# A graph layer's row gathers with an explicit index bound that skips, in place of the default check that reports

## Chip, cores and metric

One core of a Trainium2 chip runs the whole kernel. The time is device microseconds from the first to the last instruction of that core; lower is better. A core has five engines that run their own instruction queues: PE (TensorE), DVE (VectorE), ACT (ScalarE), POOL (GpSimd) and SP (SyncE), and 16 DMA engines that move the data. A DMA is issued from the queue of SP, ACT or POOL. A gather with indices (DMA_INDIRECT) is issued on POOL, which works on it while it is prepared; the data then move on the DMA engines.

## What is computed

A graph has N = 12,500 nodes with 128 features and E = 400,000 edges, sorted by their destination. Every edge has a source, a destination and 32 features.

```
h = relu(layernorm(x))                          # 12500 x 128
e = concat(h[src], h[dst], edge_attr)           # 400000 x 288
m = relu(e @ w1 + b1) @ w2 + b2                 # message of each edge
agg = segment_sum(m, dst)                       # 12500 x 128
out = x + GRU(agg, h)                           # three gates, h is the state
```

The product with the part of w1 that belongs to the source doesn't depend on the edge, so the kernel computes p = h @ w1_src once for each node and gathers rows of p. w2 is applied after the sum.

## The kernel before

**First stage.** x is read in 14 batches of 7 tiles of 128 nodes, normalised by DVE, POOL and ACT, transposed by PE, and multiplied with the source part of w1. The rows of p go to the DRAM tensor `p_rows`, which has NPAD = 12,544 rows of 128 floats (512 bytes each).

**Edge stage.** The edges are worked on in 625 groups of 640 edges; 5 groups make a chunk, and there are 125 chunks. The counter `s` (0 to 4) is the group's place in the chunk and names its buffers: `idx[:, s]`, `rows[:, s]`, `lhs[:, s]`, `onehot[:, s]`. For each group:

- SP loads 5 columns of 128 source indices into `idx` (line 310), after the gathers that used the buffer before have landed, and the edge features into `lhs` (line 333).
- POOL issues 5 gathers, one for each tile of 128 edges (`t` = 0 to 4, line 421): partition k of `rows[:, s, t]` gets the row of `p_rows` that `idx[k, s, t]` names. Ahead of the five it waits for the stored `p_rows`, for the indices (`idx_in`) and for the last reader of the buffer (`seg_ready`). POOL does nothing else in this stage. The loop over the chunks turns on POOL's own queue with register arithmetic and a branch; chunks 0 to 3 are written out ahead of it.
- DVE compares destinations with a row of numbers and so builds a one-hot matrix of the window of 95 nodes that the group's destinations lie in (`onehot`, line 788). PE transposes it (line 1001), multiplies the window's rows of h with the destination part of w1 (line 1004), and adds up destination part, edge features and bias in one product for each tile (line 1015).
- DVE adds that to the gathered rows (line 796), which is the step that waits for the gathers. ACT applies the relu (line 578), PE sums by destination with the one-hot matrix (line 1028), and DVE adds the sums to `acc` and `low` (lines 805, 806).
- The gates of 100 nodes at a time are computed between the groups, two chunks behind.

The order on each engine is written out by hand in a function `chunk` for each; the semaphores `rows_in[s]`, `pre_ready[s]`, `seg_ready[s]` and their kind hold them together.

**The other branch.** If some group's destinations don't fit the window, all engines take the branch `general()` instead, which is not executed with these inputs. Its scatter already carries `bounds_check=NPAD - 1, oob_is_err=False`, because it writes duplicates to an index beyond the tensor on purpose.

Of the kernel before, what the change touches and what calls it, by code (L numbers as in the profile page):

```python
# [17 lines left out]
NPAD = NT * P  # L18
# [39 lines left out]
def gnn_kernel(nc, x, src_cols, dst_cols, dst_rows, src_tiles, dst_tiles, ea_t, w1, b1, w2, b2, w_ih, b_ih, w_hh, b_hh, out):  # L58
# [7 lines left out]
    with ExitStack() as ctx:  # L66
        def sb(name, shape, dt=F32):
            return ctx.enter_context(nc.sbuf_tensor(name, shape, dt))
# [4 lines left out]
        def sems(name, n):  # L73
            return [sem(f"{name}{i}") for i in range(n)]
# [39 lines left out]
        idx = sb("idx", [P, G, T], I32)  # L114
# [88 lines left out]
        idx_in, ea_in, rows_in, h_win_ready = (sems(n, G) for n in ("idx_in", "ea_in", "rows_in", "h_win_ready"))  # L203
# [19 lines left out]
        def wait(eng, s, value):  # L223
            if not (isinstance(value, int) and value <= 0):
                eng.wait_ge(s, value)  # L225
# [146 lines left out]
        def _(pool):  # L372
# [35 lines left out]
            def chunk(c):  # L408
                arrived = c * 16 + 16
                if not isinstance(c, int):  # L410

                    pool.reg_add(arrived_reg, c * 16, 16)
                    arrived = arrived_reg
                for s in range(G):

                    pool.wait_ge(p_stored[1], BATCHES // 2 * 16)

                    pool.wait_ge(idx_in[s], arrived)
                    wait(pool, seg_ready[s], c)
                    for t in range(T):  # L420
                        pool.indirect_dma_start(  # L421
                            out=rows[:, s, t, :], out_offset=None, in_=p_rows[:, :],
                            in_offset=bass.IndirectOffsetOnAxis(ap=idx[:, s, t:t + 1], axis=0)).then_inc(rows_in[s], 16)


            chunk(0)

            def general():
# [14 lines left out]
                with pool.Fori(0, TILES) as t:  # L443
# [7 lines left out]
                    for gathered, (buffer, table, index) in zip(g_gathered, ((g_p, p_rows, g_src), (g_q, q_rows, g_dst), (g_sum, sum_rows, g_dst))):  # L451
# [8 lines left out]
                                            in_=g_new, in_offset=None, bounds_check=NPAD - 1,  # L460
                                            oob_is_err=False).then_inc(g_scattered, 16)
            choose(pool, lambda: over_chunks(pool, chunk, 1), general)

        @block.scalar
# [712 lines left out]
```

## Time and profile before

| | |
|---|---|
| time, median of 3 runs | 4109.21 us (4107.52 to 4110.72) |
| profiled execution, first to last instruction | 4107.6 us |
| POOL busy | 3091.0 us, 75% |
| PE busy / weight loads | 3103.1 us, 76% / 2782.6 us, 68% |
| DVE, ACT busy | 1393.9 us, 34% / 1298.5 us, 32% |
| DMA queue of POOL | 205.00 MB, 19.8% of the 16 engines' span |
| granted TensorE clock, mean | 0.839 |

Busy shares say how much an engine works, not whether it sets the time; for that the profile has the chain that ended last, which is followed back from the last instruction to what released each step. "Issue" in it is time in which the engine waited for nothing that the profile shows. The profile gives no time of the profiled execution besides its span, so the span stands for it; it lies 1.6 us below the median of the runs. Register, branch and semaphore instructions are not counted as busy.

### The profile page before, as it was taken

Reading aid. Unit: us, or ns where it says so; the run is one execution under the profiler, and the core shown is the slowest. Engines: PE = TensorE matmul, PEld = TensorE weight load, DVE = VectorE, ACT = ScalarE, POOL = GpSimd, SP = SyncE. Lnnn points to the kernel's source line nnn. Section 1 sums busy time; section 2 is a strip of 40 time slices with the busy share of each in tenths; the row PEclk is TensorE's granted clock in tenths of the full one; section 3 lists DMA queues with packets and bytes.
Section 4 is the critical chain, followed back from the end, with each engine's and each line's share of the span. In section 5 each row is a group of like instructions: output and inputs, shape, how many; then the busy total and the mean of one; then the engine's idle time right before and its main releaser. Section 6 shows DMA issues by size and latency. Waiting matters only on the chain.

```text
span 4107.6 us, 71393 instructions
## 1 busy us (share of the span) xinstructions
PE 3103.1 (76%) x20157; PEld 2782.6 (68%) x20157; DVE 1393.9 (34%) x3514; ACT 1298.5 (32%) x3575; POOL 3091.0 (75%) x3163
## 2 busy tenths in 40 slices
PE   5777777777777777777777777777777777777777
PEld 4666676666666666666666667666766666766676
DVE  5233333333333333333333333333333333333333
ACT  5323333333333333333333333333333333233332
POOL 4777777777777777777777777777777777777776
PEclk8888888888888888888888888888888888888887
DMA  6222222222222222222222222222222222222222
GB/s 184 65 67 68 67 67 67 68 68 67 68 67 67 68 68 67 68 68 68 68 68 68 67 69 67 68 69 67 68 67 67 67 68 68 68 68 67 67 68 55
DMA packets 275619, 287.98 MB, mean 70 GB/s; under 512 B 153848, under 2 KB 204697, under 8 KB 275476
## 3 DMA queue, kind: packets, MB, share of 16 engines
q0 software_dynamic: 100000, 205.00, 19.8%
q1 hardware_dynamic: 147282, 69.63, 6.0%
q10 hardware_dynamic: 28318, 13.14, 1.1%
q8 instruction: 8, 0.13, 0.0%
q14 instruction: 11, 0.08, 0.0%
HBM read 274.60 MB, written 12.83 MB: 70 GB/s over the span
## 4 chain that ended last, share of the span: by engine, by line
POOL 72%; issue 25%; DMA 1%; POOLq 1%; DVE 0%; PE 0%; ACT 0%; SPq 0%; DVEq 0%; ACTq 0%
POOL rows L421 72%; DMA p_rows<-low 1%; POOLq L225 1%; POOLq L236 0%; DMA acc<-in_x_dram 0%; DVE stats L698 0%; DVE mv L704 0%; DVE low L723 0%; PE ps L1089 0%; PE ps L1090 0%; ACT low L503 0%; DMA rows<-p_rows,idx 0%; PE ps L1028 0%; ACT hT L496 0%; SPq L263 0%
## 5 line engine op out<-in xcount | busy, mean ns | idle before, releaser
L421 POOL DMA_INDIRECT rows<-p_rows,idx x3125 | 3060.7, 979 | 963.6 <-issue 951.9
L1028 PE MATMUL ps<-onehot,rows 128*128 128x95 f32 x6250 | 984.8, 314 | 545.5 <-ACT rows L578 545.2
L1028 PEld LDWEIGHTS ps<-onehot,rows 128*128 128x128 f32 x6250 | 894.4, 223 | 641.4 <-ACT rows L578 391.3
L572 ACT ACTIVATE lhs<-ps 96x640 f32<-96x640 f32 x625 | 437.6, 700 | 2478.2 <-PE ps L1004 2475.9
L796 DVE TENSOR_TENSOR rows<-rows,ps 128x640 f32<-128x640 f32 x625 | 513.1, 821 | 1848.7 <-DMA rows<-p_rows,idx 1840.8
L1015 PE MATMUL ps<-rhs,lhs 128*128 128x128 f32 x6250 | 991.4, 316 | 178.8 <-DVE rows L796 178.3
L1015 PEld LDWEIGHTS ps<-rhs,lhs 128*128 128x128 f32 x6250 | 924.0, 230 | 209.9 <-issue 200.7
L1001 PE MATMUL ps<-ident,onehot 128*96 128x128 f32 x3125 | 565.1, 322 | 239.1 <-DVE onehot L788 236.8
L1001 PEld LDWEIGHTS ps<-ident,onehot 128*96 128x96 f32 x3125 | 401.3, 149 | 338.8 <-DVE onehot L788 328.7
L578 ACT ACTIVATE rows<-rows 128x640 f32<-128x640 f32 x625 | 459.7, 736 | 276.0 <-DVE rows L796 274.6
L788 DVE TENSOR_TENSOR onehot<-iota_w,dst_int 128x475 f32<-128x475 f32 x625 | 401.8, 643 | 39.1 <-issue 39.0
L1004 PE MATMUL ps<-w_dst,h_win 128*95 128x128 f32 x1250 | 281.8, 313 | 0.0
L1004 PEld LDWEIGHTS ps<-w_dst,h_win 128*95 128x95 f32 x1250 | 211.1, 198 | 2.0
L1040 PE MATMUL ps<-low,b2ih 1*128 (+1 forms) x738 | 189.0, 339 | 0.0
L805 DVE TENSOR_TENSOR acc<-acc,ps 128x95 f32 x625 | 158.7, 254 | 77.9 <-issue 9.4
L566 ACT COPY h_win<-hT 128x95 f32 x625 | 169.8, 272 | 7.7 <-issue 2.3
L1029 PE MATMUL ps<-ident,count 95*1 95x95 f32 x625 | 171.7, 275 | 0.0
L1039 PE MATMUL ps<-acc,w2ih 128*128 (+1 forms) x738 | 158.9, 301 | 0.0
L573 ACT COPY rhs<-ps 95x128 f32<-95x128 f32 x625 | 156.3, 250 | 0.0
L1040 PEld LDWEIGHTS ps<-low,b2ih 1*128 1x128 f32 x738 | 121.5, 205 | 41.1 <-issue 11.6
L806 DVE TENSOR_TENSOR low<-low,ps 1x95 f32 x625 | 147.1, 235 | 0.1
L832 DVE TENSOR_TENSOR out_fin<-x_fin,ps 100x128 f32<-100x128 f32 x123 | 35.5, 288 | 309.6 <-PE ps L1047 309.6
(94 smaller groups left out, 1211.4 us busy)
## 6 DMA issues: line engine op xcount, KB each, us to landing
rows<-p_rows,idx POOLq DMA_INDIRECT x3125
lhs<-in_ea_t_dram SPq DMA_DIRECT2D x625, 80.0 KB
idx<-in_src_cols_dram SPq DMA_DIRECT2D x625, 2.5 KB
p_rows<-low SPq DMA_DIRECT2D x14, 448.0 KB, 3.5
x_fin<-in_x_dram ACTq DMA_DIRECT2D x123, 50.0 KB
out_dram<-out_fin ACTq DMA_DIRECT2D x123, 50.0 KB
acc<-in_x_dram SPq DMA_DIRECT2D x13, 448.0 KB, 4.8
low<-in_dst_rows_dram SPq DMA_DIRECT2D x1, 1562.5 KB
```

The costliest lines, as they stand in the source:

```text
L421: pool.indirect_dma_start(out=rows[:, s, t, :], out_offset=None, in_=p_rows[:, :], in_offset=bass.IndirectOffsetOnAxis(ap=idx[:, s, t:t + ...
L566: nc.scalar.copy(h_win[:], hT[:, bass.ds(b, W)]).then_inc(h_win_ready[s], 1)
L572: nc.scalar.activation(lhs[0:WB, s, :], onehotT_ps, ACT.Copy, accum_out=count[:, s:s + 1])
L578: nc.scalar.activation(m, m, ACT.Relu).then_inc(message_ready[s], 1)
L788: nc.vector.tensor_tensor(onehot[:, s, :, 0:W], iota_w[:, :].unsqueeze(1).to_broadcast([P, T, W]), d.unsqueeze(2).to_broadcast([P, T, W]), ...
L796: nc.vector.tensor_tensor(r, r, pre_ps[s % 2], ALU.add).then_inc(summed[s], 1)
L1001: nc.tensor.transpose(onehotT_ps[:, t * P:(t + 1) * P], onehot[:, s, t, :], ident[:])
L1004: nc.tensor.matmul(q_ps, h_win[:], w1_dst[:], start=True, stop=True).then_inc(onehotT_ready[s], 1)
L1015: last = nc.tensor.matmul(pre_ps[s % 2][:, t * D:(t + 1) * D], lhs[:, s, t * P:(t + 1) * P], rhs[:, s, :], start=True, stop=True)
L1028: nc.tensor.matmul(sg[:, 0:W], rows[:, s, t, :], onehot[:, s, t, 0:W], start=(t == 0), stop=(t == T - 1))
L1029: nc.tensor.transpose(sg[0:1, W:2 * W], count[0:W, s:s + 1], ident[0:W, 0:W]).then_inc(seg_ready[s], 1)
L1040: last = nc.tensor.matmul(gate_ps[:, g, :], b2ih[0:1, cols], d, start=False, stop=(g == 2))
```

## The change

Each of the five gathers of a group gets two arguments: a bound on the index, 12,543, which is the last row of `p_rows`, and the order not to report an index beyond it but to leave its row out. By the interface's description, without them an index beyond the bound is an error that is reported. Indices are 0 to 12,499, so no row is left out in either form. As in the scatter of the other branch, the bound reaches the gather in a register of POOL's queue, which an instruction of that queue sets.

```
                     for t in range(T):
                         pool.indirect_dma_start(
                             out=rows[:, s, t, :], out_offset=None, in_=p_rows[:, :],
-                            in_offset=bass.IndirectOffsetOnAxis(ap=idx[:, s, t:t + 1], axis=0)).then_inc(rows_in[s], 16)
+                            in_offset=bass.IndirectOffsetOnAxis(ap=idx[:, s, t:t + 1], axis=0),
+                            bounds_check=NPAD - 1, oob_is_err=False).then_inc(rows_in[s], 16)
```

## Rows read from the trace of the kernel before

**Rows 1.** Page, part 4: chain that ended last, by engine and by line.

```profile
POOL 72%; issue 25%; DMA 1%; POOLq 1%; DVE 0%; PE 0%; ACT 0%; SPq 0%; DVEq 0%; ACTq 0%
```

**Rows 2.** Source line 421: durations, idle time before it, who waited for it.

```profile
L421 POOL DMA_INDIRECT rows<-p_rows,idx x3125: 940/944/3367, 76.8 to 4088.5; - x196
...
  issue: 951.9, 3124
...
  DVE rows L796: 1840.8, 588
```

**Rows 3.** Waits of all engines, in total, times, longest.

```profile
ACT lhs L572 <- PE ps L1004: 2475.9, 624, 9.4
DVE rows L796 <- DMA rows<-p_rows,idx: 1840.8, 588, 5.2
POOL rows L421 <- issue: 951.9, 3124, 0.3
```

**Rows 4.** Waits of SP's queue.

```profile
SPq L310 <- DMA rows<-p_rows,idx: 3290.8, 617, 6.8
```

**Rows 5.** Busy time of each engine over the edge stage.

```profile
core 0: us, PE busy (x) PEld busy (x) DVE busy (x) ACT busy (x) POOL busy (x), PEclk, DMA share, GB/s
77.00:4089.40 4012.40, 3050.63 (x19828) 2738.67 (x19829) 1338.35 (x3237) 1250.74 (x3495) 3060.48 (x3125) 0.84 0.26 68
```

**Rows 6.** Timeline of POOL, 2004 to 2020 us: start, duration, idle before.

```profile
2005.55 0.94 POOL L421 DMA_INDIRECT rows<-p_rows,idx  x1 [0.30 <-issue]
2006.79 1.42 POOL L421 DMA_INDIRECT rows<-p_rows,idx  x1 [0.30 <-issue]
2008.51 0.94 POOL L421 DMA_INDIRECT rows<-p_rows,idx  x1 [0.30 <-issue]
2009.76 0.94 POOL L421 DMA_INDIRECT rows<-p_rows,idx  x1 [0.30 <-issue]
2011.01 0.94 POOL L421 DMA_INDIRECT rows<-p_rows,idx  x1 [0.30 <-issue]
2012.26 0.94 POOL L421 DMA_INDIRECT rows<-p_rows,idx  x1 [0.30 <-issue]
2013.51 0.94 POOL L421 DMA_INDIRECT rows<-p_rows,idx  x1 [0.30 <-issue]
2014.76 0.94 POOL L421 DMA_INDIRECT rows<-p_rows,idx  x1 [0.30 <-issue]
2016.01 0.94 POOL L421 DMA_INDIRECT rows<-p_rows,idx  x1 [0.30 <-issue]
2017.25 1.41 POOL L421 DMA_INDIRECT rows<-p_rows,idx  x1 [0.30 <-issue]
```

**Rows 7.** Timeline of DVE beside the two longer gathers.

```profile
2006.75 0.65 DVE L788 TENSOR_TENSOR onehot<-iota_w,dst_int 128x475 f32<-128x475 f32 x1
...
2009.84 0.82 DVE L796 TENSOR_TENSOR rows<-rows,ps 128x640 f32<-128x640 f32 x1 [2.45 <-DMA rows<-p_rows,idx]
...
2017.21 0.63 DVE L788 TENSOR_TENSOR onehot<-iota_w,dst_int 128x475 f32<-128x475 f32 x1
```

**Rows 8.** POOL's instructions by line and shape, whole span.

```profile
L421 POOL DMA_INDIRECT rows<-p_rows,idx x3125 | 3060.7, 979 | 963.6 <-issue 951.9 <-DMA p_rows<-low 11.7
L393 POOL TENSOR_TENSOR low<-acc,rstd 128x512 f32<-128x512 f32 x14 | 14.6, 1043 | 33.0 <-DVE shift L715 33.0
...
L376 POOL IOTA iota_w<- 128x95 f32 x1 | 0.2, 212 | 0.0
...
L378 POOL IOTA floor_c<- 128x1 f32 x1 | 0.1, 121 | 0.0
...
L375 POOL MEMSET zero_col<- 128x1 f32 x1 | 0.1, 95 | 0.0
```

**Rows 9.** Tile idx: register instructions of SP's queue (durations ns, min/median/max).

```profile
L310 SPq MOVE idx<-in_src_cols_dram x605: 29/29/29, 186.6 to 4059.2; - x152
```

## Prediction

> **What bounds the kernel now.** I read the chain that ended last first. POOL's work is 72% of it and "issue" 25%; nothing else has more than 1% [rows 1]. The reader is to see that one engine carries the span, although PE is as busy by the table. Next, line 421, which is that POOL work: 3125 gathers, from 76.8 to 4088.5 us, median 944 ns, minimum 940 ns, and before 3124 of them the same kind of idle time, "issue", 951.9 us in all [rows 2]. That is 951.9 / 3124 = 0.305 us each. With the mean of 979 ns [rows 8] a gather takes 1.284 us from start to start, and 3124 x 1.284 = 4011 us is the edge stage. So the span is 76.8 (before the first gather) + 4011.7 + 0.9 (last gather) + 18.2 (the last group's sums and gates) = 4107.6 us.
>
> Then the waits, to see which way they point. DVE waited for gathered rows 588 times, 1840.8 us in all [rows 3]; SP's index loads waited for gathers to land 617 times, 3290.8 us [rows 4]. POOL waited for nobody: no semaphore is among the releasers after the first gather [rows 2, 8]. In the edge stage the DMA engines are 26% busy, DVE 33% (1338 of 4012 us), ACT 31% and PE 76% [rows 5]. Work on these others has slack behind POOL. ACT's 2475.9 us of waiting for PE [rows 3] is that slack passed on, because PE's order of work includes groups that wait for DVE's sum.
>
> What follows: the price of the change is 3125 times whatever it does to one gather. 1 ns on each is 3.1 us, and 0.2% of the time (8.2 us), which is about what a measurement of this kernel can tell from no change, is only 2.6 ns on each.
>
> **The change, part by part.**
>
> *Data moved, waits, order.* The same 128 rows of 512 bytes go to the same places with the same semaphores. No index is beyond the bound, so nothing is skipped. Cost 0. The DMA engines' 26% [rows 5] would cover it if a few descriptors differed; without that cover a gather's data would have to be slower than 1.28 us, which the share excludes.
>
> *The register.* The bound reaches the gather in a register, so POOL's queue has one more instruction for each gather, 3125 in all. The nearest row is a register move on SP's queue, 29 ns [rows 9]. Exposed in full it costs 3125 x 29 ns = 91 us. What speaks against is the gap. Of the gathers shown, the one at 2008.51 us is the first of a chunk (gather number 1500 from zero), with the loop's register arithmetic, its branch and the waits of a group ahead of it; the one at 2014.76 us is the first of a group, with the waits alone; the others have nothing between. All have 0.30 us [rows 6], and the longest of all 3124 is 0.3 us as well [rows 3]. So POOL's queue gets on with such instructions while a gather of 0.94 us is being worked on, and the cover is far larger than 29 ns. Cost 0; 91 us if the queue turns out to wait, because the gather itself needs the register.
>
> *The check inside the gather.* No row of this trace shows a gather with a bound, so this is bounded from both sides. From below: the description of the interface says that the default form checks too; then a compare of each index with a number is made already, and what changes is the number and what follows a hit, of which there is none. Cost 0, or, if one more operation is made for all indices at once, what one more column costs POOL. The two IOTAs give (212 - 121) / (95 - 1) = 0.97 ns for a column over 128 partitions [rows 8], times 3125 = 3.0 us (0.07%). From above: the indices are taken one after another, which 944 / 128 = 7.4 ns for each index allows. At the IOTA's 0.97 ns for each that is 124 ns a gather, 388 us; at TENSOR_TENSOR's 1043 / 512 = 2.04 ns it is 261 ns, 815 us. Below zero: if the reporting form carries work that the skipping form leaves out, the same prices hold with the other sign; even the whole gap of 0.305 us could belong to it (-952 us), though nothing in the rows says so. Between these ends I take the lower one, 0 to 3 us, as 1 us. The nearest thing in the rows is that a gather's work doesn't vary: its minimum and median are 4 ns apart over 3125 lists of indices [rows 2], so it depends on no index's value, as work done in the same steps for all would; and the compare replaces one.
>
> *The longer gathers.* The mean is 35 ns above the median [rows 2, 8], which is 109 us over 3125. The gather that starts at 2006.79 takes 1.42 us, beside a DVE compare of 0.65 us that started at 2006.75; the one at 2017.25 takes 1.41 us, beside the same line's 0.63 us from 2017.21 [rows 6, 7]. The gathers beside DVE's sum at 2009.84, whose second input is in PSUM, take 0.94 us. So a gather that begins just behind a DVE operation with both inputs in SBUF loses about 0.47 us. The change leaves both in place: cost 0. If it lengthened the gather by a second look at the indices, this loss could come twice. The Trainium skill, page SBUF — State Buffer, section Who interferes with whom, has this as a rule: a DVE tensor_tensor with two SBUF inputs holds off a GpSimd instruction that reads SBUF. The trace agrees with it here (1.42 us beside 0.94 us). By that rule a second read of the indices would be exposed to DVE as the first is, which is the third rival below.
>
> Sum: 0 + 0 + 1 + 0 = 1 us on 4109.2, so 4110 us.
>
> **The rivals.**
>
> *Each index is checked by itself (slower).* For it: 7.4 ns for each index leave room for steps by index. Against: a default check would make them already. It decides as soon as one index costs 2.6 / 128 = 0.02 ns more. Price 124 ns a gather, 4109 + 388 = 4497 us; at the dearer price 4924 us.
>
> *The indices are read again for the check (slower).* One mechanism: a second read of the index column before the descriptors are written, which costs nothing by itself when DVE is away but meets DVE's compare as often as the first does. Price: the 109 us again, 4218 us. If the read also cost what a whole POOL instruction of one column does (95 ns [rows 8]), 297 us more, 4515 us. The Trainium skill, GPSIMD Engine Reference, section Performance pitfalls for Q7 kernels, gives about 102 cycles for a read command that doesn't overlap its forerunner; at the 1.2 GHz that the page Trainium Kernel Development and Optimization gives for GpSimd in the Trainium skill's Quick Reference that is an estimate of 85 ns, +266 us, 4375 us. No row here shows such a read alone.
>
> *The register is waited for (slower).* For it: nothing before hands a register to a gather, so its hiding is shown only for instructions that the gather doesn't need. Against: the even gap of 0.30 us. It decides when the move is not done by the end of the gather before. 4109 + 91 = 4200 us.
>
> *The report costs something now (faster).* For it: 0.305 us of issue before each gather have no explanation in the rows. Against: the gap is there whatever precedes. Priced as one queue instruction, 29 ns, it gives 4109 - 91 = 4018 us; as a step for each index (124 ns), 3721 us. At that price a group would take 5 x 1.16 = 5.8 us, and PE's 3051 us busy over 625 groups are 4.9 us, so POOL would still set the time.
>
> *The change does nothing.* If both forms end in the same work the result is the forecast's, 4109 us.
>
> **How the numbers follow.** Forecast, nothing or nearly nothing on each gather: 0.42. Index by index: 0.18. Second read: 0.13. Register: 0.07. Faster: 0.20. So faster 0.20, same 0.42, slower 0.38. The forecast's own range is 4106 to 4114: 0 to 3 us, and the 3 us that the runs differ by. The range reaches down to 4080, which leaves out most of the faster case (0.15), and up to 4500, which holds the register, both kinds of second read but their dearest, and the step by index at its lower price; it leaves out the dearer prices (0.05). That is 0.80 inside.
>
> **What would show it.** In the changed profile: median of line 421 still 944 ns and idle before it still 0.305 us (forecast); a median up by about 124 ns (index by index); a mean that moved away from the median, with more gathers near 1.4 us, up from a 35 ns difference (second read); a gap above 0.305 us with the same median (register); a smaller gap or median (faster). DVE's wait for gathered rows would move with the gathers, 1840.8 us now, and PE's, DVE's and ACT's busy time not at all. The forecast is wrong if the default form makes no check at all: then everything in the bounded form is new work on the one engine that sets the time, and there is nothing to hide it behind.

## The result, and the profile after

| | before | after |
|---|---|---|
| median of 4 runs each, us | 4108.36 (4105.32 to 4110.72) | 4319.30 (4317.99 to 4322.88) |
| profiled execution, span, us | 4107.6 | 4321.2 |

The kernel became slower: ratio 1.0516, 95% interval 1.0502 to 1.0531, or 211 us. That is 67.5 ns on each of 3125 gathers.

First the page of the kernel after: part 4, the chain by engine and by line, and part 5, the gathers' line (times, mean ns, idle time before).

```profile
POOL 72%; issue 22%; POOLq 3%; DMA 1%; PE 1%; DVE 0%; ACT 0%; SPq 0%; DVEq 0%; ACTq 0%
POOL rows L421 72%; POOLq L421 2%; POOLq L225 0%; DMA p_rows<-low 0%; POOLq L236 0%; DMA acc<-in_x_dram 0%; DVE stats L699 0%; PE ps L960 0%; PE ps L1029 0%; DMA onehot<-base_f_dram 0%; DVE dst_int L778 0%; PE ps L1002 0%; PE ps L1090 0%; PE ps L1091 0%; DVE mv L705 0%
...
L421 POOL DMA_INDIRECT rows<-p_rows,idx x3125 | 3274.6, 1048 | 963.7 <-issue 963.4
```

Beside [rows 1] and [rows 8]: the same engine and line carry the chain. Its busy time rose from 3060.7 to 3274.6 us, by 213.9 us; its idle time stayed at 963.6 to 963.7 us. The span rose by 213.6 us. So all of the loss is inside the gathers. "POOLq" rose in the chain from 1% to 3%: that is the new register moves. It looks like a cost, but the share of "issue" fell from 25% to 22%, and the idle time before the gathers is the same. The moves are drawn into a gap that was there.

Then the line's own view (duration ns, minimum/median/maximum).

```profile
L421 POOLq MOVE  x3125: 29/29/29, 75.6 to 4286.1; - x196
L421 POOL DMA_INDIRECT rows<-p_rows,idx x3125: 993/1000/3374, 76.5 to 4302.0; - x196
...
  issue: 963.4, 3124
...
  DVE rows L797: 2168.6, 621
```

Against [rows 2] the median rose from 944 to 1000 ns and the minimum from 940 to 993 ns. So nearly every gather does 56 ns more work: 56 x 3125 = 175 us. The mean rose by 68 to 69 ns (979 to 1048), 12 to 13 ns more than the median, which makes the other 39 us of the 213.9. The idle time is as it was, in spite of a move of 29 ns ahead of each gather. DVE waits longer for its rows (2168.6 against 1840.8 us), as the prediction said it would if the gathers grew.

Where the 39 us lie is seen in the timelines of POOL and of DVE, at the same place as [rows 6, 7].

```profile
2007.18 1.00 POOL L421 DMA_INDIRECT rows<-p_rows,idx  x1 [0.30 <-issue]
2008.49 1.53 POOL L421 DMA_INDIRECT rows<-p_rows,idx  x1 [0.31 <-issue]
2010.33 1.00 POOL L421 DMA_INDIRECT rows<-p_rows,idx  x1 [0.30 <-issue]
...
2014.24 1.00 POOL L421 DMA_INDIRECT rows<-p_rows,idx  x1 [0.30 <-issue]
2015.55 1.43 POOL L421 DMA_INDIRECT rows<-p_rows,idx  x1 [0.30 <-issue]
```

```profile
2008.35 0.23 DVE L807 TENSOR_TENSOR low<-low,ps 1x95 f32 x1
2008.51 0.63 DVE L789 TENSOR_TENSOR onehot<-iota_w,dst_int 128x475 f32<-128x475 f32 x1
...
2015.31 0.23 DVE L807 TENSOR_TENSOR low<-low,ps 1x95 f32 x1
2015.47 0.63 DVE L789 TENSOR_TENSOR onehot<-iota_w,dst_int 128x475 f32<-128x475 f32 x1
```

The long gathers again start within a tenth of a us of DVE's compare (line 788 before, 789 after). Counted over both whole timelines, 288 gathers before and 393 after were more than 0.05 us above the median, by 0.38 us and 0.39 us on average. So a collision costs what it did; there are 105 more of them, and 105 x 0.39 = 41 us, which is about the 39.

The same timelines show what a collision is. Of the gathers that begin in the first 0.4 us of a compare, 209 of 211 were long before and 357 of 360 after. Before, the later they began the less they lost: by the medians 0.48 us in the first tenth of a us, then 0.37, 0.27 and 0.18. So the gather waits until the compare of 0.65 us is nearly over. Of those that begin in the first 0.4 us of DVE's sum (line 796 before, 797 after), which has one input in PSUM, none was long: 134 before, 228 after.

### The profile page after: what moved, and what is told of

Same layout as the page of the kernel before. It is cut to its first block, busy times and chain, and to the rows that moved or that the text cites. A ratio compares the mean times of both kernels' runs of the same rounds, so it can differ in the third digit from the quotient of the medians.

```text
span 4321.2 us, 74518 instructions
## 1 busy us (share of the span) xinstructions
PE 3176.3 (74%) x20157; PEld 2855.7 (66%) x20157; DVE 1397.9 (32%) x3514; ACT 1307.4 (30%) x3575; POOL 3305.0 (76%) x3163
## 3 DMA queue, kind: packets, MB, share of 16 engines
q0 software_dynamic: 100000, 205.00, 17.8%
## 4 chain that ended last, share of the span: by engine, by line
POOL 72%; issue 22%; POOLq 3%; DMA 1%; PE 1%; DVE 0%; ACT 0%; SPq 0%; DVEq 0%; ACTq 0%
POOL rows L421 72%; POOLq L421 2%; POOLq L225 0%; DMA p_rows<-low 0%; POOLq L236 0%; DMA acc<-in_x_dram 0%; DVE stats L699 0%; PE ps L960 0%; PE ps L1029 0%; DMA onehot<-base_f_dram 0%; DVE dst_int L778 0%; PE ps L1002 0%; PE ps L1090 0%; PE ps L1091 0%; DVE mv L705 0%
## 5 line engine op out<-in xcount | busy, mean ns | idle before, releaser
L421 POOL DMA_INDIRECT rows<-p_rows,idx x3125 | 3274.6, 1048 | 963.7 <-issue 963.4
L797 DVE TENSOR_TENSOR rows<-rows,ps 128x640 f32<-128x640 f32 x625 | 513.4, 821 | 2175.6 <-DMA rows<-p_rows,idx 2168.6
L1016 PE MATMUL ps<-rhs,lhs 128*128 128x128 f32 x6250 | 1028.0, 324 | 247.4 <-DVE rows L797 246.8
L1016 PEld LDWEIGHTS ps<-rhs,lhs 128*128 128x128 f32 x6250 | 961.1, 238 | 281.6 <-issue 273.7
L1002 PE MATMUL ps<-ident,onehot 128*96 128x128 f32 x3125 | 589.1, 332 | 231.8 <-DVE onehot L789 230.3
L1002 PEld LDWEIGHTS ps<-ident,onehot 128*96 128x96 f32 x3125 | 422.9, 155 | 325.3 <-DVE onehot L789 313.6
L1005 PE MATMUL ps<-w_dst,h_win 128*95 128x128 f32 x1250 | 292.8, 324 | 0.0
L1005 PEld LDWEIGHTS ps<-w_dst,h_win 128*95 128x95 f32 x1250 | 220.3, 206 | 2.3
L1043 PE MATMUL ps<-hT,whh_sb 128*128 (+1 forms) x492 | 128.6, 347 | 0.0
```

What stands on the lines that cost most here:

```text
L421: pool.indirect_dma_start(out=rows[:, s, t, :], out_offset=None, in_=p_rows[:, :], in_offset=bass.IndirectOffsetOnAxis(ap=idx[:, s, t:t + ...
L797: nc.vector.tensor_tensor(r, r, pre_ps[s % 2], ALU.add).then_inc(summed[s], 1)
L1002: nc.tensor.transpose(onehotT_ps[:, t * P:(t + 1) * P], onehot[:, s, t, :], ident[:])
L1005: nc.tensor.matmul(q_ps, h_win[:], w1_dst[:], start=True, stop=True).then_inc(onehotT_ready[s], 1)
L1016: last = nc.tensor.matmul(pre_ps[s % 2][:, t * D:(t + 1) * D], lhs[:, s, t * P:(t + 1) * P], rhs[:, s, :], start=True, stop=True)
```

## The experiments

Each ratio is against the kernel before, run on the same chip, where it took 4097.2 us (beside runs 1, 3, 4 and 12), 4089.8 us (5 to 8) and 4096.8 us (2, 9 to 11).

**1. The bound with the report.**

```
-                            bounds_check=NPAD - 1, oob_is_err=False).then_inc(rows_in[s], 16)
+                            bounds_check=NPAD - 1).then_inc(rows_in[s], 16)
```

> The bound of 12,543 stays, the order to skip silently goes: an index beyond would be reported, as before. Theory A (the bound itself is new work inside the gather: median 944 ns before, 1000 ns after, whatever follows a hit): median 1000 ns and about 4319 us, as after the change. Theory B (the silent skipping is the work, and a bound that reports is what the default form has): median 944 ns and about 4109 us.

Measured: 4357.31 us, ratio 1.0634 (1.0617 to 1.0652). The line's view:

```profile
L421 POOL DMA_INDIRECT rows<-p_rows,idx x3125: 1006/1010/3541, 77.4 to 4337.1; - x196
```

Theory B falls: a bound that reports is not what the default form has. It is slower by 66 ns a gather, and silent skipping takes 10 ns of that off (13 ns against run 3, on the same chip). Theory A had the mechanism but not those 10 ns.

**2. Silent skipping without a bound.**

```
-                            in_offset=bass.IndirectOffsetOnAxis(ap=idx[:, s, t:t + 1], axis=0)).then_inc(rows_in[s], 16)
+                            in_offset=bass.IndirectOffsetOnAxis(ap=idx[:, s, t:t + 1], axis=0),
+                            oob_is_err=False).then_inc(rows_in[s], 16)
```

> The kernel before with the order not to report alone, and no bound. Theory A (the bound is the new work; it cost 56 ns a gather with silent skipping and 66 ns with reporting): median 944 ns and the time of the kernel before, ratio 1.000. Theory E (not reporting takes work out of the gather, 10 ns as between the two bounded forms): median 934 ns, 31 us less, ratio 0.992.

Measured: 4094.97 us, ratio 0.9998 (0.9988 to 1.0007). The line's view:

```profile
L421 POOL DMA_INDIRECT rows<-p_rows,idx x3125: 940/944/3572, 76.6 to 4079.3; - x196
```

Median and minimum are those of before to the nanosecond. Whether the report is asked for costs something only where there is a bound. Together with run 1: the bound is the new work, and the default form takes none of its time. Whether the default form looks for an index beyond the tensor at all is not shown, since no run gave it one.

**3. One register for all gathers.**

```
+            bound_reg = pool.alloc_register("bound")
+            pool.reg_mov(bound_reg, NPAD - 1)
...
-                            bounds_check=NPAD - 1, oob_is_err=False).then_inc(rows_in[s], 16)
+                            bounds_check=bound_reg, oob_is_err=False).then_inc(rows_in[s], 16)
```

> The bound and the silent skip stay as after the change, but the bound is put into one register once, ahead of the edge stage, so the 3125 register moves go (29 ns each on POOL's queue). Theory A (work inside the gather): median 1000 ns, about 4319 us, no change against the changed kernel. Theory C (the queue waits for the move): 0.944 us and 4109 us, or at least 91 us (3125 x 29 ns) of the 211 us back, 4228 us.

Measured: 4310.63 us, ratio 1.0525 (1.0508 to 1.0543), which overlaps the changed kernel's 1.0502 to 1.0531. The line's view (it is line 423 here) and its row by shape (times, mean ns, idle before):

```profile
L423 POOL DMA_INDIRECT rows<-p_rows,idx x3125: 992/997/3778, 76.5 to 4287.2; - x196
```

```profile
L423 POOL DMA_INDIRECT rows<-p_rows,idx x3125 | 3259.2, 1043 | 964.3 <-issue 964.3
```

The 3124 moves that went (71,394 instructions against 74,518) gave nothing back that can be told, and the idle time stayed at 964 us. The median of 997 ns, 3 below the changed kernel's, is no sign of them either: runs 6 and 11 have the moves and 997 ns as well. Theory C falls: the moves are hidden.

**4. The moves alone.**

```
                     for t in range(T):
+                        pool.reg_mov(spare_reg, NPAD - 1)
                         pool.indirect_dma_start(
```

> The kernel before with one register move in front of each gather, into a register that no gather reads, and no bound. Theory A: the move hides under the gather before, median 944 ns, gap 0.305 us, 4109 us. Theory C (the queue's extra instruction costs): up to 4200 us if its 29 ns are exposed, 4319 us if it is the whole cause.

Measured: 4097.83 us, ratio 0.9998 (0.9988 to 1.0008). But this says nothing of the moves. The profile counts 71,393 instructions, as before the change, and has no MOVE row on POOL's queue: a move into a register that nobody reads was dropped from the program. What it shows is that the kernel before repeats to within 0.1%. Run 3 is the one that answers the question.

**5 and 6. Both forms without most of DVE's compare.**

```
-                nc.vector.tensor_tensor(onehot[:, s, :, 0:W], iota_w[:, :].unsqueeze(1).to_broadcast([P, T, W]),
-                                        d.unsqueeze(2).to_broadcast([P, T, W]), ALU.is_equal).then_inc(onehot_ready[s], 1)
+                w = W if isinstance(c, int) and c == 0 else 1
+                nc.vector.tensor_tensor(onehot[:, s, :, 0:w], iota_w[:, 0:w].unsqueeze(1).to_broadcast([P, T, w]),
+                                        d.unsqueeze(2).to_broadcast([P, T, w]), ALU.is_equal).then_inc(onehot_ready[s], 1)
```

> The kernel before, which leaves out most of the one-hot build: after the first chunk only one of 95 columns of each one-hot matrix is compared (128x5 in place of 128x475), so the sums are not the reference's. No bound. Theory D (the excess of the mean over the median of 944 ns, 109 us, is the gathers held off by that compare): mean falls to about 945 ns and the time to about 4000 us. The rival (the excess comes from the DMA engines' descriptor rings or another load): mean stays at 979 ns, 4109 us.

> The changed kernel with the same part of the one-hot build left out. Theory A with D (56 ns of new work in each gather, 175 us, and 35 us more collisions with the compare by where the gathers come to lie): mean falls from 1048 to about 1001 ns and the time to about 4175 us, so that bound against no bound costs 175 us here, not 211 us. The rival (the check reads the indices a second time and a part of the 56 ns is waiting for DVE): the difference to the same kernel without a bound shrinks well below 175 us.

Measured: without a bound 4004.84 us, ratio 0.9794 (0.9776 to 0.9813); with it 4164.87 us, ratio 1.0186 (1.0167 to 1.0206). POOL's row by line and shape, without a bound and then with it:

```profile
L421 POOL DMA_INDIRECT rows<-p_rows,idx x3125 | 2955.0, 946 | 963.8 <-issue 951.7 <-DMA p_rows<-low 11.7 <-PE ps L1030 0.3
```

```profile
L421 POOL DMA_INDIRECT rows<-p_rows,idx x3125 | 3116.7, 997 | 963.9 <-issue 963.9
```

In both the mean has come down to the median (944 and 997 ns, to within 2 ns). Theory D holds: the excess of the mean over the median is made by the compare. Without collisions the bound costs 997 - 946 = 51 ns a gather, 160 us, which is the 160.0 us between the two medians. So of the 211 us about 160 to 175 are work in the gather, and the rest is collisions. The difference came out 15 us below the 175 expected; with a median that is 53 to 56 ns higher with the compare and without it, the new work is not waiting for DVE.

**7 to 10. Fewer indices.** 64 rows without and with a bound are runs 7 and 8, 32 rows without and with are 9 and 10. The gathers take 64 or 32 of 128 rows, without a bound and with it; a memset of `rows` ahead of the first gather, with a wait for it, is the only other edit. The edit of run 7:

```
-                            out=rows[:, s, t, :], out_offset=None, in_=p_rows[:, :],
-                            in_offset=bass.IndirectOffsetOnAxis(ap=idx[:, s, t:t + 1], axis=0),
+                            out=rows[0:64, s, t, :], out_offset=None, in_=p_rows[:, :],
+                            in_offset=bass.IndirectOffsetOnAxis(ap=idx[0:64, s, t:t + 1], axis=0),
```

> The kernel before, which gathers 64 of the 128 rows of each tile: the other 64 stay as they were, so the sums are not the reference's. No bound. Only the gather's duration is read, since the other engines may set the time. All theories: the part of 944 ns that grows with the number of indices halves; if all of it does, median 472 ns, if none, 944 ns.

> The changed kernel, which gathers 64 of the 128 rows of each tile, beside the same without a bound. If the check is made index by index (0.44 ns for each of 128, 56 ns), the bound costs half, 28 ns, at 64 indices. If it is a fixed step of the instruction (reading the bound, one compare of a whole vector), it costs 56 ns at 64 indices as well.

> The kernel before, which gathers 32 of 128 rows of each tile, the others stay, so the sums are not the reference's. From 944 ns at 128 and 903 ns at 64 indices (0.64 ns an index, 862 ns fixed): median 883 ns.

> The changed kernel with 32 of 128 rows gathered. The bound cost 56 ns at 128 indices and 39 ns at 64: if that is a line (0.27 ns an index and 22 ns fixed), it costs 30 ns at 32, median 913 ns; if it is a step for each block of indices, it stays near 39 ns or halves to 20 ns.

One execution each: 3963.05 and 4139.74 us at 64 rows, 3871.89 and 4028.30 us at 32. The line's view of each: 64 without, 64 with, 32 without, 32 with a bound.

```profile
L422 POOL DMA_INDIRECT rows<-p_rows,idx x3125: 899/903/4082, 78.2 to 3942.2; - x196
```

```profile
L422 POOL DMA_INDIRECT rows<-p_rows,idx x3125: 937/942/3593, 79.5 to 4118.9; - x196
```

```profile
L422 POOL DMA_INDIRECT rows<-p_rows,idx x3125: 862/867/3714, 79.0 to 3851.4; - x196
```

```profile
L422 POOL DMA_INDIRECT rows<-p_rows,idx x3125: 907/911/3250, 79.2 to 4008.8; - x196
```

| indices | median without, ns | with, ns | the bound, ns |
|---|---|---|---|
| 128 | 944 | 1000 (997 in runs 3, 6 and 11) | 56 (53) |
| 64 | 903 | 942 | 39 |
| 32 | 867 | 911 | 44 |

Two things follow. A quarter of the indices leaves 92% of a gather's time: 96 indices fewer save 77 ns, 0.8 ns for each on average, so most of the 944 ns is a fixed price of the instruction. It is no straight line: the step from 128 to 64 indices saves 0.64 ns an index, the one from 64 to 32 saves 1.1, and the 883 ns expected for 32 indices were 867. And the bound's price is mostly fixed too: 39 to 44 ns at 32 and 64 indices, 53 to 56 ns at 128. At 64 indices neither side was right, since index by index gave 28 ns and a fixed step 56 ns. At 32 the line through 56 and 39 ns gave 30 ns, which was wrong too; a price that stays near 39 ns came closest to the 44 measured. A compare made index by index is excluded as the main part; at 32 indices it would have left 14 ns of 56.

**11. A bound that half of the indices are beyond.**

```
-                            bounds_check=NPAD - 1, oob_is_err=False).then_inc(rows_in[s], 16)
+                            bounds_check=N // 2 - 1, oob_is_err=False).then_inc(rows_in[s], 16)
```

> The changed kernel with a bound of 6249, so that about half of the 400,000 indices are beyond it and their rows aren't gathered; the sums are not the reference's. If the check is a step that all indices take alike and a row that is left out still has its place in the lists: median 1000 ns, about 4319 us, and POOL's queue moves about half of the bytes. If a row beyond the bound takes another way (its descriptors left out or made empty one by one): the duration moves with the number of rows left out, faster by up to 64 x 0.64 = 41 ns (what 64 indices less cost without a bound), or slower.

Measured: 4303.35 us, ratio 1.0504 (1.0486 to 1.0521). The kernel has the same memset of `rows` as runs 7 to 10. The page's row of the DMA queue (packets, MB, share of 16 engines) and the line's view:

```profile
q0 software_dynamic: 100000, 103.43, 9.8%
```

```profile
L422 POOL DMA_INDIRECT rows<-p_rows,idx x3125: 992/997/3728, 79.3 to 4283.9; - x196
```

Half the bytes (103.43 against 205.00 MB) and a median of 997 ns, as in runs 3 and 6. The number of packets, 100,000, says nothing of the rows left out: the queue has the same number in runs 7 to 10, which ask for 64 or 32 rows (102.60 and 51.40 MB). The gather works the same time whether an index is within the bound or not, and halving the transfer changes nothing, since POOL does not wait for it.

**12. The compare in another form.** The two profiles pointed to the collisions as time to be had without the change, so this run starts from the kernel before.

```
-                nc.vector.tensor_tensor(onehot[:, s, :, 0:W], iota_w[:, :].unsqueeze(1).to_broadcast([P, T, W]),
-                                        d.unsqueeze(2).to_broadcast([P, T, W]), ALU.is_equal).then_inc(onehot_ready[s], 1)
+                for t in range(T):
+                    last = nc.vector.tensor_scalar(onehot[:, s, t, 0:W], iota_w[:, :],
+                                                   dst_rel[:, bass.ds(c * (G * T) + s * T + t, 1)], None, ALU.is_equal)
+                last.then_inc(onehot_ready[s], 1)
```

> The kernel before with the one-hot matrix built by five DVE tensor_scalar operations of 128x95, one for each tile, in place of one tensor_tensor of 128x475 whose two inputs are in SBUF. Theory D (a gather is held off by a DVE operation with two inputs in SBUF, at its first tenth of a us, 109 us in all): a tensor_scalar has one tensor input, the long gathers of 1.4 us vanish, and the time is about 4000 us. The rival (any long DVE operation on SBUF holds the gather off, by the port pair for reads and writes that it takes in its fast mode): the long gathers stay or become more, 4109 us or above.

Measured: 4044.28 us, ratio 0.9872 (0.9856 to 0.9889), 1.3% below the kernel before. The gathers' row of the page:

```profile
L421 POOL DMA_INDIRECT rows<-p_rows,idx x3125 | 2997.3, 959 | 963.8 <-issue 951.8
```

The mean is 959 ns against a median of 944, so 15 ns x 3125 = 47 us of 109 remain. Neither side was right: the long gathers neither vanished nor stayed. The timelines of POOL and of DVE show what is left:

```profile
1026.20 0.94 POOL L421 DMA_INDIRECT rows<-p_rows,idx  x1 [0.30 <-issue]
1027.45 1.22 POOL L421 DMA_INDIRECT rows<-p_rows,idx  x1 [0.30 <-issue]
```

```profile
1027.42 0.24 DVE L808 TENSOR_TENSOR low<-low,ps 1x95 f32 x1
1027.58 0.96 DVE L789 TENSOR_SCALAR onehot<-iota_w,dst_int 128x95 f32<-128x95 f32 x5
```

This gather loses 0.28 us in place of up to 0.5. It began 0.13 us ahead of the row of five, and so did most that lost: of the 252 gathers that begin 0.02 to 0.25 us ahead of a row, 158 are long, by up to 0.38 us, which makes 40 of the 47 us. Their loss is the shorter the later they begin, as if they waited for the end of the first operation (259 ns by their median) and not for the whole row. Of the 331 that begin inside a row only 36 are long, by at most 0.12 us. The Trainium skill, SBUF — State Buffer, section Who interferes with whom, says that a DVE tensor_scalar can take the port pair shared with GpSimd when it runs in a two-port mode. The losses at the head of a row would fit that, the gathers inside a row do not; no run here shows which mode the operations ran in, or why these gathers go on almost unharmed. Nor does this run tell whether the shorter operation or its other form is what helps, since both changed.

## Why the prediction was right in its range and wrong in its likeliest case

**What bounds the kernel** held. All of the 213.6 us by which the span grew is in line 421's busy time (213.9 us), and 1 ns a gather was 3.1 us, as said.

**Data moved, waits, order: 0.** Held. The queue moves the same 205.00 MB. The forecast that PE's busy time would not move was wrong (3103.1 us before, 3176.3 after, at a granted clock of 0.839 and 0.824), but POOL sets the time in both.

**The register: 0.** Held, by run 3. The even gap of 0.30 us [rows 6] was the right row to read: POOL's queue gets its own instructions done while a gather runs, also one that the next gather needs.

**The range.** The forecast was 4110 us, and "slower" had 0.38 against 0.42 for "same". That 4319 us lie within 4080 to 4500 is owed to the width that the rivals gave the range. None of them had this price, which lies between their 4218 and 4375 us, and the likeliest case was 209 us off. The number in the range is luck as far as the mechanism goes.

**The check inside the gather: 0 to 3 us, taken as 1.** This is the step that failed. It measured 160 us (without collisions, runs 5 and 6) to 175 us (56 ns by the medians). I took the interface's description, "an error that is reported", for work that the default form does. Runs 1 and 2 show that without a bound the order to report changes nothing (944 ns, ratio 0.9998), while a bound that reports costs 66 ns. What the last paragraph of the prediction named as its weak point fits what happened: what the bounded form does for its bound is all new work. Whether the default form makes its check elsewhere or not at all is open. I also used the evenness of the durations (940 to 944 ns) as evidence for a compare that is there already. It is no such evidence: the bounded form is as even, 993 to 1000 ns.

**The upper bounds** rested on 944 / 128 = 7.4 ns an index. That was a wrong reading too: an index costs about 0.8 ns, and the rest is fixed. The rival "each index is checked by itself" had the right place and sign, but its 388 us were more than twice the 160 to 175 us measured for the work in the gather, and the runs with fewer indices show that the price is mostly one step for the whole gather.

**The longer gathers: 0.** Wrong by about 40 us. I let the collisions with DVE stay as they were, since neither operation changed. But which gathers start beside a compare depends on how the two engines' turns fall together. With a gather of 1.305 us from start to start (1000 ns and the gap) in place of 1.249 us it was 393 in place of 288. The bounded forms with 128 rows all had more (371, 414 and 438 in runs 3, 1 and 11), the unbounded repeats all fewer (266 and 260 in runs 2 and 4).

The timelines of DVE show where the new ones come from. First a sum and the compare after it, before the change ([rows 6, 7] have the sum of 2009.84 us and the gathers), then the sum ahead of the compare of 2008.51 us, after it:

```profile
2011.09 0.63 DVE L788 TENSOR_TENSOR onehot<-iota_w,dst_int 128x475 f32<-128x475 f32 x1
```

```profile
2007.26 0.82 DVE L797 TENSOR_TENSOR rows<-rows,ps 128x640 f32<-128x640 f32 x1 [2.55 <-DMA rows<-p_rows,idx]
```

The sum starts when gathered rows have landed, so it keeps step with the gathers; in both cases it starts 0.08 us behind the start of one. The compare follows 1.25 us behind the sum. That is just the old distance between gathers: before, the next gather had begun 0.08 us ahead of the compare (2011.01) and took 0.94 us. The new distance is 0.056 us longer, and the gather at 2008.49 begins 0.02 us ahead of the compare and is caught. About 250 of the 625 compares follow a sum in this way. Beside them 115 gathers were long before and 223 after; beside the others it was 171 and 169. So the new collisions are these.

The prediction also took the gathers beside the sum at 2009.84 us for a sign that an input in PSUM does no harm. That row could not show it, as the gather began 0.08 us ahead of the sum, where a compare does no harm either; the counts over the whole timeline show it (none of 134 long).

The rival "the indices are read again" gave 4218 us with a median that stays; the median rose, and without the compare the bound's price stayed at 51 ns, so a second exposed read is not what it is. Nor did the stretch of time grow in which a gather is caught, from 0.05 us ahead of a compare to 0.45 us into it: 263 of the 288 long gathers begin in it before, 388 of the 393 after. The 102 cycles that the Trainium skill, GPSIMD Engine Reference, section Performance pitfalls for Q7 kernels, gives for one read command, an estimate of 85 ns as in the prediction, lie above the 39 to 56 ns of the whole check; no run here times such a read.

**What stays open.** Of the 39 to 56 ns, how much is taking over the bound from the register and how much is comparing. No run separates the two. Why the price is 53 to 56 ns at 128 indices and about 40 at 64 and at 32 is open as well.

## What to carry to other kernels

Where POOL's gathers set the time, an option of a gather is paid on each of them, and a description of what the default does is no evidence of what it costs: leave the bound off where indices are known to fit. Look at the mean of such a line against its median: a gap between them can be another engine in the way. Here it was, and five short tensor_scalar operations in place of one long tensor_tensor took 1.3% off. Ask also how the turns of two engines will fall when one gets a little longer; a loss of 56 ns by work drew about 13 ns of collisions after it, because an operation of DVE that keeps a fixed distance to the landed rows came to meet the next gather.

## What the runs showed of the hardware that was not expected

- A gather of 32 rows takes POOL 867 ns and one of 128 rows 944 ns: the fixed part is nearly all of it.
- A row beyond the bound saves POOL nothing (997 ns with half of the rows left out), though the queue moves half of the bytes (103.43 against 205.00 MB).
- The queue's number of packets does not follow the rows: 100,000 for 3125 gathers of 128, 64 or 32 rows each.
- With a bound, the silent form is 10 to 13 ns shorter than the one that reports (1000 and 997 against 1010 ns), though no index was beyond it in either.
- A gather that begins in the first 0.4 us of a DVE TENSOR_TENSOR of 0.65 us with both inputs in SBUF waits until that is nearly over (357 of 360 long), and beside one with an input in PSUM it does not (none of 228).
